# The scan's first projection moved into the tail of the soft mixture, and the late decays spread over the scan's first steps

## The chip, the cores and the metric

One core of a Trainium2 chip runs the whole program. The metric is the device time of one execution in microseconds. The kernel was timed in three runs; a fourth execution was profiled, and all rows of the trace come from that one.

## What is computed

The reference is two blocks of a network on x of shape (2, 2048, 256), in float32. Block 0 is attention and a soft mixture of experts. Block 1 is a state-space layer (Mamba-2) and an expert-choice mixture. Each is modulated by shift, scale and gate rows of a conditioning vector. What matters here is the end of the soft mixture and the beginning of the state-space layer:

```python
h = _layernorm(x) * (1 + ca) + sa          # then the layer's own norm
zxbcdt = u @ W_in + b_in                   # 1160 columns: z 512, xs 512, B 64, C 64, dt 8
dt = softplus(zxbcdt[..., -8:] + dt_bias); A = -exp(A_log)
decay = exp(dt * A)
h = decay * h + (dt * xs) B^T ; y = h C    # a scan over 2048 positions
y = (y + D * xs) * silu(z)
x = x + ga * (y @ W_out + b_out)
```

## The kernel before, in words

The work runs in 32 tiles of 128 positions, 16 for each of two batches. Each phase is one block in which every engine has its own written-out instruction list; engines wait for each other on semaphores. Between two blocks stands a barrier, at which all engines and the DMAs that the block waits for have ended.

**Soft mixture** (`soft_mixture`). For batch 1, a loop over turns t = 0 to 15 combines the experts' outputs for tile t: PE does eight products (`combine`, L1665, seen as 16 matmul records), DVE adds them into x and takes statistics (`update`, L1176 to L1181). PE may begin turn t when DVE has updated tile t-2. Between the turns the rows for the scan are made for pairs of tiles, eight pairs, numbered 0 to 7:

- DVE `row_stats` (L1189 to L1197), POOL `power` (L1037), DVE `state_rows` (L1209 to L1223) into a row buffer of the pair's parity, POOL a second power (L1046), DVE `state_offset` (L1229), ACT `state_normed` (L1469), PE `state_turn` (L1674, the transposes of the pair), ACT `state_turned` (L1482), SP `turned_out` (L971, to DRAM), PE `state_steps` (L1683, the step size matmuls), DVE `step_sizes` (L1236, which empties the buffer that the next use but one needs).
- the residual, which also uses the row buffer: POOL in three operations (L1052 to L1056, semaphore u_x) for pairs 0 to 5 of batch 1, DVE in three operations (`residual`, L1317 to L1321) for pairs 6 and 7. `state_rows` of a pair waits until the pair before the last, which has the same buffer, has its residual.
- the tail after turn 15: step matmuls of pair 4, then turn and steps of pairs 5, 6 and 7.

The decays of the scan's tiles (softplus, cumulative sums, exponentials) are made in three parts. The first 16 tiles are done in turns 0 to 5. The second part, the first two tiles of batch 1, is begun in turn 8 (`log_ratio`), turn 10 (`decay_sizes` on DVE, `cumulate` on PE, L1693), turn 13 (`keep_sums`), 14 (`turn_sums`, L1700) and 15 (`keep_turned`, L1310). The remaining 14 tiles, the "late" ones, are done in the scan's block before its loop.

**Scan** (`state_space`). Step n handles job n: tile n // 2 of batch n % 2. For each job PE does `project` (L2331 on: three outputs pbc, px, pz with 128, 512 and 512 columns, each of six exact matmuls and one for the bias, L2337), `states`, `state_rows`, `within`, `correlate` and `outputs`. ACT splits the input tile (`high`, L1979), empties the projection (`evacuate`, L1985 to L1989) and computes the decays' exponentials (`decay`, L2006 and L2009) from rows that SP fetches (`stage`, L1896 to L1898: cs, et and a broadcast of 512 KB, cumb). DVE subtracts the low half (`low`, L2107), gates, masks and updates the state. The order on each engine is written out by hand: before the loop come both first tiles, project(0) and all late decays (ACT `late_exp`, `late_log`, `late_sums`; DVE `late_ratio`, `late_sizes`, `late_kept`; PE `late_cumulate`, L2419). SP's list is: two small loads, stage(0), stage(1), the first and third quarter of uT (L1884, 1 MB each), the modulation rows (768 KB), the gate weights (L1915), three shared weight matrices (512 KB each), the other two quarters, the late cumulative sums out (L1921), and then stage(n) from n = 2. ACT negates the gate weights (L2072) before its loop. In the loop ACT's list of step n begins with high(n+2) and evacuate(n+1), and has decay(n+1) after them.

## Time and profile before

| | us |
|---|---|
| median of 3 runs | 1760.3 |
| lowest and highest run | 1756.54, 1760.31 |
| the profiled execution, from outside | 1759.81 |
| its span in the trace | 1758.1 |
| PE busy (matmul) | 1642.9, 93% |
| PE weight loads | 1383.2, 79% |
| DVE busy | 1209.1, 69% |
| ACT busy | 732.0, 42% |
| POOL busy | 544.9, 31% |

Busy time is a sum over the span; an engine's idle time costs something only where others wait for it. The mean granted clock of PE is 0.98 of its full 2.4 GHz. In the rows, a line of a timeline begins with start and duration in us; "[3.87 <-DVE d_f_dA L1294]" says that the engine was idle for 3.87 us before it and which instruction released it. SPq rows are the issues of DMAs, not the transfers.

### The profile page before, as it was taken

The page shows a single profiled execution, that of the slowest core. Times are in us where ns is not written, and L with a number is a line of the kernel's source. Part 1 is how long each engine was busy: PE and PEld are TensorE (multiplying, and loading weights), DVE is VectorE, ACT ScalarE, POOL GpSimd, SP SyncE. Part 2 cuts the span into 40 slices and gives each one's busy share as a digit, 9 for nine tenths or more (in the row PEclk, how much of TensorE's full clock was granted, in tenths as well). Part 3 has the DMA queues.
Part 4 walks back from the last instruction along what each step waited for, and adds up shares of the span by engine and source line. Part 5 has one row for each costly group of instructions (what it writes and reads, how often), then busy time and mean ns, then how long its engine had stood idle before and what let it go on. Part 6 is the DMA issues. An engine that isn't in the chain of part 4 may idle for free. (4 is left out here: it accounts for less than half of the span.)

```text
span 1758.1 us, 25512 instructions
## 1 busy us (share of the span) xinstructions
PE 1642.9 (93%) x9248; PEld 1383.2 (79%) x9248; DVE 1209.1 (69%) x2662; ACT 732.0 (42%) x1443; POOL 544.9 (31%) x446
## 2 busy tenths in 40 slices
PE   6999989989999999979987999999989999999996
PEld 4788878888867888856876888888768787888895
DVE  6877678764435655636686899999967845666663
ACT  3333333343324234424525666666621224444442
POOL 2100020000000003222252666666600023777764
PEclk9999999999999999989987999999999999999998
DMA  6000000010010000020116122232141123656553
GB/s 221 4 1 1 1 1 1 1 49 1 1 48 1 1 13 13 29 95 26 52 33 209 61 76 76 76 87 81 63 145 60 60 60 119 171 134 171 132 128 37
DMA packets 80248, 111.55 MB, mean 63 GB/s; under 512 B 15982, under 2 KB 60154, under 8 KB 79868
## 3 DMA queue, kind: packets, MB, share of 16 engines
q1 hardware_dynamic: 66172, 91.43, 16.1%
q0 software_dynamic: 12288, 17.31, 5.5%
q8 instruction: 75, 1.23, 0.3%
q10 hardware_dynamic: 1664, 1.18, 0.2%
q14 instruction: 49, 0.40, 0.1%
HBM read 81.59 MB, written 27.68 MB: 62 GB/s over the span
## 5 line engine op out<-in xcount | busy, mean ns | idle before, releaser
L2915 POOL DMA_INDIRECT out<-k_eo,idx x64 | 117.3, 1832 | 75.4 <-DVE k_eo L3007 60.7
L1816 POOL DMA_INDIRECT k_xe<-rows_dram,idx x64 | 82.5, 1289 | 178.8 <-DVE idx L2848 140.7
L1665 PE MATMUL d_pO<-d_sp,d_raw 128*128 128x257 f32 x512 | 116.6, 385 | 2.8 <-ACT d_raw L1460 2.7
L1665 PEld LDWEIGHTS d_pO<-d_sp,d_raw 128*128 128x128 f32 x512 | 96.9, 192 | 18.1 <-ACT d_raw L1460 3.5
L537 ACT ACTIVATE b_p<-b_pS,b_nmax 128x2048 f32<-128x2048 f32 (+14 forms) x32 | 40.6, 1270 | 141.2 <-DVE b_nmax L678 141.2
L61 PE MATMUL b_pO<-b_vh,b_ph 128*128 128x256 f32 x302 | 88.0, 291 | 4.4 <-DVE b_pl L660 4.3
L62 PE MATMUL b_pO<-b_vh,b_pl 128*128 128x256 f32 x302 | 85.7, 284 | 0.0
L63 PE MATMUL b_pO<-b_vl,b_ph 128*128 128x256 f32 x302 | 85.5, 283 | 0.0
L333 POOL TENSOR_TENSOR x<-x,b_vrow 128x256 f32<-128x256 f32 x32 | 24.0, 782 | 187.8 <-DVE b_hs L606 187.7
L2006 ACT ACTIVATE g_dlm<-g_cumb,g_cs 128x128 f32<-128x128 f32 x256 | 78.4, 393 | 2.5 <-DMA g_cumb<-cum_dram 2.5
L1441 ACT COPY d_raw<-d_pL 128x512 f32<-128x512 f32 x64 | 37.4, 588 | 93.4 <-PE d_pL L63 93.4
L2966 ACT ACTIVATE k_act_g<-k_pg 128x512 f32<-128x512 f32 x64 | 38.3, 598 | 88.5 <-PE k_pu L63 88.5
L61 PE MATMUL k_po<-k_wh,k_hh 128*128 128x256 f32 x256 | 72.4, 283 | 2.1 <-issue 2.1
L3020 DVE TENSOR_TENSOR k_hid<-k_act_g,k_pu 128x512 f32<-128x512 f32 x64 | 44.1, 688 | 44.1 <-ACT k_act_g L2966 43.5
L669 DVE TENSOR_REDUCE b_part<-b_pS 128x1 f32<-128x512 f32 (+3 forms) x86 | 53.1, 624 | 28.5 <-PE b_pS L63 28.2
L63 PE MATMUL k_po<-k_wl,k_hh 128*128 128x256 f32 x256 | 72.5, 283 | 0.0
L62 PE MATMUL k_po<-k_wh,k_hl 128*128 128x256 f32 x256 | 72.4, 283 | 0.0
L61 PE MATMUL b_pS<-b_kh,b_qh 128*128 128x512 f32 (+3 forms) x172 | 70.0, 407 | 1.4 <-DVE b_vl L652 1.4
L660 DVE TENSOR_TENSOR b_pl<-b_pT,b_ph 128x512 fp32r<-128x512 f32 (+3 forms) x86 | 50.4, 619 | 25.1 <-ACT b_ph L529 25.0
L1620 PE MATMUL d_pO<-o_vals,mod 128*128 128x256 f32 x256 | 63.7, 393 | 4.1 <-ACT mod L1446 4.1
L2606 ACT ACTIVATE i_act_g<-i_pg 128x512 f32<-128x512 f32 x30 | 17.9, 598 | 114.2 <-PE i_pu L63 112.1
L63 PE MATMUL b_pS<-b_kl,b_qh 128*128 128x512 f32 (+3 forms) x172 | 64.9, 377 | 0.0
(568 smaller groups left out, 5336.8 us busy)
## 6 DMA issues: line engine op xcount, KB each, us to landing
g_cumb<-cum_dram SPq DMA_DIRECT2D x32, 512.0 KB, 4.2
k_wf<-in_WgT SPq DMA_DIRECT2D x16, 512.0 KB
k_wf<-in_WuT SPq DMA_DIRECT2D x16, 512.0 KB
k_wf<-in_WdT SPq DMA_DIRECT2D x16, 512.0 KB
rows_dram<-h_hx SPq DMA_DIRECT2D x32, 136.0 KB, 3.9
x<-in_x SPq DMA_DIRECT2D x8, 512.0 KB, 9.5
d_w<-in_w SPq DMA_DIRECT2D x4, 1024.0 KB, 6.2
uT_dram<-d_ug SPq DMA_DIRECT2D x16, 256.0 KB, 2.4
```

The lines of the kernel that those rows point to most:

```text
L61: nc.tensor.matmul(out, ah, bh, start=start, stop=False)
L62: nc.tensor.matmul(out, al, bh, start=False, stop=False)
L63: return nc.tensor.matmul(out, ah, bl, start=False, stop=stop)
L537: nc.scalar.activation(pr[:, n % 2, 0:w], pS[:, bank[n]:bank[n] + w], ACT.Exp, bias=nmax[:, n % 2:n % 2 + 1], scale=scale, accum_out=esum[ ...
L660: nc.vector.tensor_tensor(pl[:, r, 0:w], src[:, 0:w], ph[:, r, 0:w].bitcast(F32), ALU.subtract).then_inc(s["lo_done"], 1)
L669: nc.vector.reduce_max(part[:, n % 2, g:g + 1], pS[:, bank[n] + g * GW:bank[n] + g * GW + width(n, g)], axis=AX).then_inc(s["part_done"], 1)
L1620: last = nc.tensor.matmul(pO[:, et % 2, 0:C], eT[g % 2][:, j * P:(j + 1) * P], xn[g * GT + j], start=g == 0 and j == 0, stop=g == NG - 1 a ...
L1665: last = nc.tensor.matmul(pO[:, t % 2, 0:PW], raw[e][:, t * P:(t + 1) * P], proc[e], start=e == 0, stop=e == E - 1)
L1816: nc.gpsimd.indirect_dma_start(out=m.xe[:, e % 2, t, :], out_offset=None, in_=m.rows, in_offset=bass.IndirectOffsetOnAxis(ap=column(m, e, ...
L2006: nc.scalar.activation(le[:, b, h, :], cumb[:, b, h, :], ACT.Relu, bias=cs[:, b, 3, h:h + 1], scale=-1.0).then_inc(s["dd_done"], 1)
L2915: nc.gpsimd.indirect_dma_start(out=out, out_offset=bass.IndirectOffsetOnAxis(ap=column(m, e, t), axis=0), in_=eo[:, e % 2, t, :], in_offse ...
L3020: nc.vector.tensor_tensor(hid[:, f % 2], act_g[:, f % 2], pu[:, f % 2], ALU.mult).then_inc(s["hid_done"], 1)
```

## The change

Four things are changed.

1. **First projection.** project(0), its split into halves, and stage(0) leave the scan. The mixture does them: ACT `first_high` after pair 3's rows, DVE `first_low` at turn 13, PE `first_projection` in three parts in the tail, one of 7 matmuls with 128 columns after pair 5's turn, one of 7 with 512 columns after pair 6's turn, one of 7 with 512 after pair 6's steps. SP issues the three DMAs of stage(0) (`first_stage`) after pair 4's turned rows. Four PSUM banks (pL) are kept for both blocks.
2. **Third row buffer.** Pair 5 of batch 1 gets a buffer of its own. Its residual moves from POOL to DVE, in three parts between the operations of the tail; pair 7's rows wait for pair 3's residual.
3. **Second part of the decays.** `cumulate` moves from turn 10 to 12, `keep_sums` from 13 to 14, `turn_sums` from 14 to 15, `keep_turned` from turn 15 into the tail.
4. **Scan.** The late decays are spread over steps 0 to 3; each projection output waits for its own buffer only; project(1) has correlate(0) between its first and second output; SP fetches the modulation rows after stage(3), and the quarters of uT, the gate weights and the shared matrices before stage(2); ACT negates the gate weights in step 3; two memsets are smaller or later.

The core of the diff:

```diff
+        first_h, first_l = [placed(n, [P, CH, P], area + k * KB, FR) for k, n in enumerate(("first_h", "first_l"))]
+        m.cumb = placed("cumb", [P, B, HEADS, P], area + 30 * KB - 512)
-        pL = ps("d_pL", [P, T])
+        pL = m.pL
+        third = placed("uh_third", [P, 2, C], area + 10 * KB)
+        rows_of = lambda b, q: third[:] if b and q == PAIRS - 3 else uh_[b][:, q % 2]
...
+            def first_stage():
+                sp.wait_ge(s["o_ready"], B * NTB)
+                sp.wait_ge(s["f_kept"], 1)
+                sp.wait_ge(s["f_out"], 16)
+                sp.wait_ge(s["f_turned"], 2)
+                sp.dma_start(m.csb[:, 0], m.cs[:, 0]).then_inc(s["bb_in"], 16)
+                sp.dma_start(m.etb[:, 0], m.etot[:, 0]).then_inc(s["bb_in"], 16)
+                sp.dma_start(m.cumb[:, 0].rearrange("p h t -> p (h t)"),
+                             m.cum_dram[0:HEADS, :].rearrange("h t -> (h t)").partition_broadcast(P)).then_inc(s["bb_in"], 16)
             for q in range(PAIRS):
                 turned_out(1, q)
+                if q == PAIRS - 4:
+                    first_stage()
...
-                    if b and q >= PAIRS - 2:
+                    if b and q >= PAIRS - 3:
                         continue
...
-                if n >= 2:
+                if b and q == PAIRS - 1:
+                    dve.wait_ge(s["u_x"], n - 3)
+                elif n >= 2:
                     dve.wait_ge(s["u_x"], n - 1)
...
-                        if t in (3, 13):
-                            keep_sums(t // 13)
-                        if t in (5, 15):
-                            keep_turned(t // 15)
+                        if t in (3, 14):
+                            keep_sums(t // 14)
+                        if t == 5:
+                            keep_turned(0)
+                        if t == 13:
+                            first_low()
...
             step_sizes(1, PAIRS - 4)
+            residual(PAIRS - 3, 0)
             state_rows(1, PAIRS - 1)
             step_sizes(1, PAIRS - 3)
+            residual(PAIRS - 3, 1)
             state_offset(1, PAIRS - 1)
+            keep_turned(1)
+            residual(PAIRS - 3, 2)
+            step_sizes(1, PAIRS - 2)
             for q in range(PAIRS - 2, PAIRS):
-                residual(q)
-                step_sizes(1, q)
+                for i in range(3):
+                    residual(q, i)
+            step_sizes(1, PAIRS - 1)
...
-                        if t in (2, 10):
-                            cumulate(t // 10)
-                        if t in (4, 14):
-                            turn_sums(t // 14)
+                        if t in (2, 12):
+                            cumulate(t // 12)
+                        if t in (4, 15):
+                            turn_sums(t // 15)
+            def first_projection(part):
+                if part == 0:
+                    pe.wait_ge(s["winl"], CH + 1)
+                    pe.wait_ge(s["winh"], CH + 3)
+                    pe.wait_ge(s["f_cumT"], 1)
+                    pe.wait_ge(s["f_kept"], 2)
+                bank_of, o, width = ((2, ZX, 2 * STATE), (1, INNER, INNER), (0, 0, INNER))[part]
+                dst = pL[:, bank_of * GW:bank_of * GW + width]
+                for k in range(CH):
+                    exact_matmul(nc, dst, first_h[:, k, :], first_l[:, k, :], m.winh[:, k, o:o + width], m.winl[:, k, o:o + width], k == 0, False)
+                nc.tensor.matmul(dst, m.onesr[:], m.bb[:, o:o + width], start=False, stop=True)
             for kind, q in tail:
                 if kind == "u":
                     state_turn(1, q)
+                    if q < PAIRS - 1:
+                        first_projection(q - PAIRS + 3)
                 else:
                     state_steps(1, q)
+                    if q == PAIRS - 2:
+                        first_projection(2)
@@ scan, SP @@
-            stage(0)
             stage(1)
             inputs(0)
             inputs(2)
-            sp.wait_ge(s["f_chain"], 9)
-            sp.dma_start(m.mod[:, :, SB:GB + 1, :].rearrange("p b m c -> p b (m c)"),
-                         m.mod_dram[1][:, SB:GB + 1, :].rearrange("b m c -> b (m c)").partition_broadcast(P)).then_inc(s["mods_in"], 16)
             sp.dma_start(gw[:], w["gate_wT"].rearrange("(h p) n -> p h n", p=P)).then_inc(s["gate_in"], 16)
             for dst, src in ((m.wg, w["Ws_gT"]), (m.wu, w["Ws_uT"]), (m.wd, w["Ws_dT"])):
                 sp.dma_start(dst[:], src.rearrange("(h p) n -> p h n", p=P)).then_inc(s["shared_in"], 16)
             inputs(1)
             inputs(3)
+            stage(2)
+            stage(3)
+            sp.wait_ge(s["f_chain"], 9)
+            sp.dma_start(m.mod[:, :, SB:GB + 1, :].rearrange("p b m c -> p b (m c)"),
+                         m.mod_dram[1][:, SB:GB + 1, :].rearrange("b m c -> b (m c)").partition_broadcast(P)).then_inc(s["mods_in"], 16)
+            stage(4)
             sp.wait_ge(s["f_cumT"], 1)
             sp.dma_start(m.cum_dram[late.start * HEADS:late.stop * HEADS, :], cumT[0:NL, :]).then_inc(s["f_out"], 16)
-            for n in range(2, LAST):
+            for n in range(5, LAST):
@@ scan, ACT @@
-            high(0)
             high(1)
-            late_exp()
-            late_log()
-            decay(0)
             act.wait_ge(s["zeroed"], 1)
             evacuate(0)
             by_state(0)
-            late_sums()
-            act.wait_ge(s["gate_in"], 16)
-            nc.scalar.mul(minus_gw[:], gw[:], -1.0).then_inc(s["gate_done"], 1)
+            decay(0)
+            late_exp()
             for n in range(LAST):
...
+                if n == 2:
+                    late_sums()
                 if is_job(n + 1):
                     decay(n + 1)
+                if n == 1:
+                    late_log()
+                if n == 3:
+                    negated_gate()
@@ scan, DVE @@
-            low(0)
             low(1)
-            late_ratio()
-            late_sizes()
+            nc.vector.memset(H[:], 0.0)
             gates(0)
+            nc.vector.memset(by_tile, 0.0)
             masked(0)
-            late_kept()
             for n in range(LAST):
-                if n == 1:
-                    late_turned()
...
+                if n == 2:
+                    late_kept()
                 if is_job(n):
                     sums(n)
+                if n == 3:
+                    late_turned()
...
+                if n == 0:
+                    late_ratio()
+                if n == 1:
+                    late_sizes()
@@ scan, PE @@
-                pe.wait_ge(s["ul_done"], n + 1)
-                pe.wait_ge(s["bc_copied"], n)
-                pe.wait_ge(s["zr_done"], n)
-                pe.wait_ge(s["xs_copied"], n)
-                for dst, o, width in ((pbc, ZX, 2 * STATE), (px, INNER, INNER), (pz, 0, INNER)):
+                pe.wait_ge(s["ul_done"], n)
+                for dst, o, width, freed in ((pbc, ZX, 2 * STATE, "bc_copied"), (px, INNER, INNER, "xs_copied"), (pz, 0, INNER, "zr_done")):
+                    pe.wait_ge(s[freed], n)
+                    if n == 4 and freed == "bc_copied":
+                        pe.wait_ge(s["f_kept"], 1)
+                    if n == 1 and freed == "xs_copied":
+                        correlate(0)
...
-            project(0)
-            late_cumulate()
             await_bc(0)
             state_rows(0)
-            correlate(0)
             for n in range(LAST):
                 if is_job(n + 1):
                     project(n + 1)
-                if n == 0:
-                    late_turn()
-                if n == 1:
-                    pe.wait_ge(s["f_cumT"], 1)
+                if n == 2:
+                    late_cumulate()
...
                     states(n)
+                if n == 3:
+                    late_turn()
```

## Rows read from the trace of the kernel before

**Rows 1.** Busy time by stretch: us, PE, PEld, DVE, ACT, POOL, granted clock, DMA share, GB/s
```profile
845.00:917.00 72.00, 67.69 (x334) 58.82 (x334) 60.71 (x192) 22.68 (x43) 35.27 (x32) 0.95 0.10 31
917.00:934.00 17.00, 7.53 (x33) 6.62 (x32) 11.11 (x40) 5.45 (x11) 2.15 (x4) 0.55 0.14 48
934.00:957.00 23.00, 17.96 (x81) 13.93 (x82) 13.21 (x29) 13.79 (x38) 6.58 (x6) 0.81 0.85 294
957.00:987.00 30.00, 30.00 (x191) 25.05 (x190) 25.79 (x43) 18.98 (x49) 17.34 (x17) 1.00 0.29 95
```
**Rows 2.** Timeline of PE from turn 10 to the tail: start, duration, instruction, idle before
```profile
893.01 0.61 PE L1693 MATMUL d_pL<-d_f_dA,d_upto 128*128 128x16 f32 x2 [3.87 <-DVE d_f_dA L1294]
...
912.15 3.64 PE L1665 MATMUL d_pO<-d_sp,d_raw 128*128 128x257 f32 x16
915.64 0.95 PE L1683 MATMUL d_pT<-mod,d_ug 128*128 128x8 f32 x8
...
921.14 1.88 PE L1683 MATMUL d_pT<-mod,d_ug 128*128 128x8 f32 x8 [4.06 <-DVE mod L1236]
```
**Rows 3.** Groups of DVE instructions, 893.9 to 920.9: busy, mean ns, idle before
```profile
L1176 DVE RECIPROCAL d_crs<-d_pO 128x1 f32<-128x1 f32 x5 | 0.8, 162 | 3.1 <-PE d_pO L1665 3.1
```
**Rows 4.** Timeline of DVE, rows of pairs 6 and 7
```profile
913.31 2.61 DVE L1209 SCALAR_TENSOR_TENSOR d_uh<-x,mean,d_umod 128x256 f32<-128x256 f32 x2
...
918.72 0.28 DVE L1310 COPY d_cumT<-d_pL 16x128 f32<-16x128 f32 x1
...
921.80 0.88 DVE L1209 SCALAR_TENSOR_TENSOR d_uh<-x,mean,d_umod 128x256 f32<-128x256 f32 x2 [0.72 <-issue]
...
924.47 0.17 DVE L1236 TENSOR_TENSOR mod<-d_pT,mod 128x16 f32<-128x16 f32 x1
925.37 0.16 DVE L1229 SCALAR_TENSOR_TENSOR mod<-mod 128x2 f32<-128x2 f32 x1 [0.72 <-POOL mod L1046]
925.45 0.68 DVE L1317 TENSOR_TENSOR d_uh<-d_uh,d_ubout 128x512 f32<-128x512 f32 x1
```
**Rows 5.** Timeline of POOL, residual of pair 5, second of three operations
```profile
914.31 1.33 POOL L1054 TENSOR_TENSOR d_uh<-d_uh,d_umod 128x512 f32<-128x512 f32 x1
```
**Rows 6.** Timeline of SP's DMA issues over the border
```profile
929.04 0.51 SPq L971 DMA_DIRECT2D uT_dram<-d_ug  x1
933.79 0.35 SPq L1878 DMA_DIRECT2D g_neg<-in_A_log  x1
...
938.28 1.22 SPq L1884 DMA_DIRECT2D uT<-uT_dram  x2
```
**Rows 7.** Timeline of PE, the scan's start
```profile
936.13 0.47 PE L61 MATMUL g_pbc<-d_winh,g_uh 128*128 128x128 f32 x1 [5.13 <-DVE g_ul L2107]
...
943.27 0.37 PE L2419 MATMUL g_py<-g_fdA,d_upto 128*128 128x112 f32 x2
...
956.57 0.30 PE L61 MATMUL g_pbc<-d_winh,g_uh 128*128 128x128 f32 x1 [0.30 <-DVE g_wide L2112]
...
960.68 0.60 PE L2358 MATMUL g_pyT<-ident,g_wide 128*128 128x128 f32 x4
...
966.47 0.22 PE L61 MATMUL g_pbc<-d_winh,g_uh 128*128 128x128 f32 x1
```
**Rows 8.** Timeline of ACT, the scan's start
```profile
936.55 1.28 ACT L2039 ACT_TABLE_LOAD   x1
...
952.16 0.23 ACT L2072 ACTIVATE h_mgw<-h_gw 128x32 f32<-128x32 f32 x1 [5.95 <-DMA h_gw<-in_gate_wT]
...
964.70 2.46 ACT L2006 ACTIVATE g_dlm<-g_cumb,g_cs 128x128 f32<-128x128 f32 x8 [1.08 <-DMA g_cumb<-cum_dram]
```
**Rows 9.** Timeline of DVE, the last of the four late size operations
```profile
939.59 0.28 DVE L2222 SCALAR_TENSOR_TENSOR g_fdA<-d_cs,g_neg 128x112 f32<-128x112 f32 x1
```
**Rows 10.** Instructions on tile uT, 930 to 975: its four loads
```profile
DMA to landing us min/median/max: 7.0/11.9/14.4
```
**Rows 11.** The page's DMA issues: count, KB each, median us to landing
```profile
g_cumb<-cum_dram SPq DMA_DIRECT2D x32, 512.0 KB, 4.2
```

79 lines of the change are left out of this document (52 added, 27 removed).

## The prediction

> **What bounds the kernel now.** I went from the stretches to the engines' timelines around the border between the soft mixture and the scan, because every edit lies there. The stretches [rows 1] show the late turns of the mixture (845 to 917) with PE busy 67.7 of 72 us and DVE 60.7, the border (917 to 934) with PE busy 7.5 of 17 us at a granted clock of 0.55, the scan's start (934 to 957) with PE at 18.0 of 23 us, a clock of 0.81 and the DMA engines at 0.85 and 294 GB/s, and then the scan proper with PE busy 30.0 of 30. So PE is the bound of the scan and nothing there can be won by better order; the 40 us between 917 and 957 are where time is loose.
>
> The PE timeline [rows 2] shows two waits before the border: 3.87 us until 893.01 (the decay sums of turn 10 wait for DVE's step sizes) and 4.06 us until 921.14 (the step size matmuls of pair 5 wait until DVE has emptied the buffer of pair 4, L1236). Behind the second stands DVE's lateness, so I read DVE. From 893.9 to 920.9 it was idle 3.1 us, all of it ahead of L1176 waiting for PE's combinations [rows 3], which are late because of the first PE wait. And pair 6's rows (L1209 to L1223) took from 913.31 to 918.72, 5.41 us, while POOL ran the residual of pair 5 [rows 4, 5]; pair 7's same work, with POOL at rest, took from 921.80 to 924.47, 2.67 us.
>
> The border itself ends with a DMA: the last turned rows are issued at 929.04 and the next block's first instruction comes at 933.79 [rows 6]. Call that moment S. From S, PE starts project(0) at 936.13, begins the late sums at 943.27, and begins project(2) at 956.57 [rows 7]: 22.8 us after S. From there steps follow at PE's pace.
>
> **The change, part by part.** A: turns 10 to 15. Cumulate moves from turn 10 to 12, so PE no longer waits at 893.01; its three pairs of matmuls (0.61 for the first [rows 2], estimated 1.3 together) stay. DVE's idle 3.1 us goes, if PE keeps ahead: it can begin turn 11's combination near 891, and five combinations at 3.5 (912.15 to 915.64 [rows 2]) with two pair turns, one set of step matmuls and the sums are some 21 us, so turn 15's is ready near 912; DVE comes to it near 913. Pair 5's residual leaves POOL (that is what the third buffer allows: pair 7 waits for pair 3 instead of 5), so pair 6's rows run at pair 7's price: 5.41 - 2.67 = 2.7 us less. The first tile's low half costs DVE an estimated 0.4 us (128x256; 0.68 for 128x512 [rows 4]), the copy that moved (0.28, 0.2 of it not overlapped [rows 4]) leaves. Sum for A: -3.1 - 2.7 + 0.4 - 0.2 = **-5.6 us** until pair 7's rows begin. ACT's first high half is about as long and free, since ACT is busy 22.7 of those 72 us [rows 1]; without that cover it is 0.4.
>
> B: the tail (921.80 to S). DVE has nine residual thirds of 0.68 us [rows 4] where it had six. The first two new ones fill the two waits of 0.72 us [rows 4] for POOL's powers; the third, with the moved copy, adds 0.9 us behind the offset of pair 7, where DVE has slack until the last step sizes. PE gets the first projection: 7 matmuls of 128 columns and 14 of 512, 4.1 us in all at the full clock (project(2), 956.57 to 960.68 [rows 7]). Parts 0 and 1 lie in PE's waits for DVE (4.06 us before 921.14 [rows 2], and the time until the next step sizes). Part 2 stands before pair 7's turn and delays it by some 0.4 us, which the faster clock gives back (the step matmuls cost 1.88 us at the lower of its two levels, 1.2 GHz, and 0.95 at the upper, 2.4 GHz [rows 2]). SP issues three more DMAs after turn 15 (1.7 us), ahead of pair 5's turned rows, which are not ready then. I take **0** for B; with the clock at its lower level it is +5 (rival 1).
>
> C: from S to project(2), before 22.8 us. Gone are project(0), the late sums and the three DMA issues of stage 0. What ends last now? ACT's queue is high(2), then evacuate(1); high(2) needs the first quarter of uT. That DMA was issued 4.5 us after S behind eight others, 0.56 each [rows 6]; with three fewer it goes out at S + 2.8. Its kind took 7.0 us at least, 11.9 in the middle [rows 10]; it is the first of four, so I take 7.0: S + 9.8. PE's project(1) starts near S + 1.5 behind two small transposes, at the lower clock it takes 7 us (project(0) did, from 936.13 to 943.27 [rows 7]): S + 9. So the DMA ends last by a little. From high(2) to project(2) it was 4.4 us before (952.16 to 956.57, where ACT had waited 5.95 us for the gate weights [rows 8], a wait that the moved negation takes off this place). Project(2) then starts at S + 14.2: **-8.6 us**. Ends: -9.4 if the quarter lands sooner, since PE's projection then ends last, and -3.7 if it takes 11.9.
>
> D: the late decays in steps 0 to 3. DVE's seven ratio operations (some 2 us) fall in step 0, where it waits for PE. The sizes (four of 0.28, 1.2 in all [rows 9]) end step 1 and wait for ACT's logarithm, which is queued behind decay(2), and that waits for stage 2's rows. Stage 2 is now issued behind all four quarters of uT and three weight matrices, 6.1 MB; at 294 GB/s [rows 1] they are through some 21 us after S + 2, that is 9 us after project(2) starts. Its rows land then, or in the usual 4.2 us [rows 11], so decay(2) starts 7 to 9.6 us after project(2) (8.1 before, 964.70 [rows 8]), takes 2.46 and an exponential of 1, then the table load 1.28 and the logarithm 0.3: the sizes are ready 13.4 to 15.9 us after project(2) starts. Late cumulate stands behind project(3), which starts 9.9 and ends 14.0 us after project(2) starts [rows 7]. PE waits 0 to 1.9 us and spends some 0.9 (three pairs, 0.37 for the first [rows 7], with the next operation's start). Step 2's kept sums (0.9 on DVE) hold project(4) up to 0.5 us more. The late rows go out at the end of step 3, so stage 5 comes some 5 us later than now; ACT and DVE have 3 us of slack there. Sum for D: +1.4 to +3.6, taken at **+2.4**.
>
> On the table load, the row shows 1.28 us at 936.55 and ACT's next operation at once behind it [rows 8]. The Trainium skill (ScalarE: Activation LUTs, What ACT_TABLE_LOAD costs) adds a drain of 1.38 us to each switch of sets; by that, D would be 1.4 us more and the total 1749.4. No row here shows such a drain, so the sum goes without it.
>
> A + B + C + D = -5.6 + 0 - 8.6 + 2.4 = -11.8. The profiled execution took 1759.81 us outside and 1758.1 in its span, 0.5 under the median of 1760.3; 1759.8 - 11.8 = **1748.0**.
>
> **Rivals.** 1. The clock falls in the tail all the same. For: it fell to 0.55 there [rows 1] after a wait, and the new waits of about 1 us between projection parts remain. Against: three parts fill most of the idle time. Then parts 1 and 2 take 3 us each and stand before pair 6's steps and pair 7's turn, and B is +5: 1753.
>
> 2. PE's wait at turn 10 only moves. For: cumulate now stands behind pair 3's steps, and pair 5 of the mixture's rows on DVE is still slowed by POOL. Against: the step sizes it needs are written at turn 10, two turns earlier. DVE keeps its 3.1 us of idle and A is -2.5: 1751. That is the case in which this edit doesn't do what it says.
>
> 3. The quarter of uT lands at the middle of its kind, 11.9 us, or stage 2 sits behind the bulk as long again: C is -3.7: 1753. The Trainium skill (DMA: Bandwidth & Descriptors, Queues, rings and completion order) says that an engine takes descriptors in ring order, which would put stage 2 behind the bulk; the sum above already reaches to that end.
>
> 4. The removal of POOL's residual gives nothing. The rows show L1209's two operations at 2.61 us beside POOL's and 0.88 without [rows 4, 5], which is one instance of each. The mechanism would have to be another (the memory of x, say), and A would be -2.9: 1750.7. The Trainium skill (Perfetto Trace Analysis, Optimizing Scalar/DVE Operations) says that GpSimd and VectorE share a read port, so that moving work between the two might not help; by that warning the gain would be nothing, by the rows it is 2.7.
>
> 5. Slower than before. PE arrives in the scan cold and, with project(0) gone, waits for the late quarter of uT in step 0 so long that it stays at the lower clock through the first three steps. A step holds 9.9 us of PE (956.57 to 966.47 [rows 7]); matmuls at the lower clock took twice as long [rows 2], with waits between them less, so each such step costs 7 to 8 us. The point from which it decides is two and a half steps: then C's loss to -3.7 and +22 give 1775. Against: the granted clock averaged 0.81 from 934 to 957 and 1.00 from 957 on [rows 1], though PE came cold and waited there before too.
>
> **How the numbers follow.** Forecast 0.60, rival 1 0.12, rival 2 0.08, rival 3 0.10, rival 4 0.05, slower 0.05. A measurement of this kernel tells about 0.3%, 5.3 us, from no change: faster is below 1755.0, slower above 1765.6. The forecast's own ends are -15.1 (A 1.5 better, C at -9.4, D at +1.4) and -8.0 (C at -6, D at +3.6). Two rivals together land between 1755 and 1759, so some 0.10 falls within 0.3%. The range that holds 8 in 10 is 1743 to 1756: the lower end is 1.7 below the best sum for a B that gains, the upper takes in rivals 1 to 4 and part of their pairs.
>
> **What would show it.** In the profile after: no wait of PE over 1.5 us at turns 10 to 12; L1209 and L1214 for pair 6 below 0.9 us for two; the last turned rows issued near 923.4 instead of 929.04; a clock of 1.0 until the border (rival 1 if 0.5); project(2) some 14 us after the block's start, and ACT there waiting for uT and not for the gate weights; a PE wait of up to 2 us ahead of the late sums behind project(3); the rest of the scan at 9.9 us and more a step as before. If S comes not at least 4 us earlier, A is wrong; if project(2) comes later than S + 17, C is.

## The result and the profile after

The kernel after took 1755.8 us in the median of its 15 runs (1750.4 to 1761.5), the kernel before 1760.3 in 15 runs beside it (1756.5 to 1766.5): a ratio of 0.9972, with a 95% interval of 0.9960 to 0.9985. That is 4.5 us less where 12.3 were forecast (1760.3 to 1748.0). The profiled execution of the kernel after took 1755.81 outside and 1754.0 in its span.

The stretches of the kernel after, in the columns of [rows 1], with the edges moved to its own border:

```profile
845.00:917.00 72.00, 68.57 (x349) 59.64 (x349) 63.65 (x212) 24.56 (x46) 33.03 (x31) 0.98 0.12 39
917.00:931.00 14.00, 9.60 (x39) 7.52 (x39) 8.59 (x22) 3.16 (x7) 1.30 (x2) 0.67 0.17 58
931.00:945.00 14.00, 12.25 (x53) 9.79 (x54) 8.43 (x13) 9.61 (x29) 6.11 (x6) 0.72 0.78 275
945.00:965.00 20.00, 16.15 (x90) 13.02 (x90) 14.02 (x30) 10.06 (x23) 7.78 (x10) 0.94 0.55 200
```

The border is 14 us long instead of 17, and the scan's start is shorter; but from 945 to 965, right behind the start of project(2), PE is busy 16.15 of 20 us, where before it was busy all the time behind the start of project(2) (30.0 of 30 us from 957 on [rows 1]). There a large part of the gain is given back.

Absolute times before turn 9 differ by some us between executions of the same kernel, so I set one mark there, the start of output_low(1) in turn 9 (889.00 before, 888.50 after), and read each stage from it. Stages in us; S is the first DMA issue of the scan block, "states(1)" PE's first matmul of it, "last" PE's last matmul g_pi<-g_H of the scan:

```
                     mark to      pair 7's   S to       states(1)  mark
                     pair 7's     rows       states(1)  to last    to last
                     rows         to S
before                32.80       11.99      27.33      310.12     382.24
after                 28.74       13.90      17.95      317.93     378.52
after, profiled again 28.74       13.89      19.13      315.58     377.34
difference (first)    -4.06       +1.91      -9.38      +7.81       -3.72
difference (again)    -4.06       +1.90      -8.20      +5.46       -4.90
forecast (A B C D)    -5.6         0         -8.6       +2.4       -11.8
```

The stages give -3.7 in one execution and -4.9 in the other, the median of all runs -4.5. They account for the result. The first two stages repeat within 0.03 us in every execution whose code is the same there. The last two do not: S to states(1) moved by 1.2 us and states(1) to the last by 2.4 between the two executions of the kernel after. Now the four parts in the rows.

**Part A.** One of DVE's groups in the kernel after, 893.9 to 917.2 (busy, mean ns, idle before), against [rows 3]:

```profile
L1193 DVE RECIPROCAL d_crs<-d_pO 128x1 f32<-128x1 f32 x5 | 0.8, 159 | 0.0
```

and DVE's timeline, against [rows 4]:

```profile
901.83 1.88 DVE L1228 SCALAR_TENSOR_TENSOR d_uh_third<-x,mean,d_umod 128x256 f32<-128x256 f32 x2
903.63 2.90 DVE L1233 SCALAR_TENSOR_TENSOR d_uh_third<-d_uh_third,rstd,d_umod 128x256 f32<-128x256 f32 x2
...
907.52 0.42 DVE L1279 TENSOR_TENSOR d_first_l<-d_u,d_first_h 128x256 fp32r<-128x256 f32 x1
...
911.17 0.86 DVE L1228 SCALAR_TENSOR_TENSOR d_uh<-x,mean,d_umod 128x256 f32<-128x256 f32 x2
911.95 0.87 DVE L1233 SCALAR_TENSOR_TENSOR d_uh<-d_uh,rstd,d_umod 128x256 f32<-128x256 f32 x2
...
915.91 0.68 DVE L1342 TENSOR_TENSOR d_uh_third<-d_uh_third,d_ubout 128x512 f32<-128x512 f32 x1
917.24 0.88 DVE L1228 SCALAR_TENSOR_TENSOR d_uh<-x,mean,d_umod 128x256 f32<-128x256 f32 x2 [0.66 <-issue]
```

The 3.1 us of idle time ahead of the combinations are 0.0, and pair 6's rows take 2.65 us (911.17 to 913.82) instead of 5.41. Both are as forecast. But pair 5's rows, one pair earlier, now take 5.69 us (901.83 to 907.52); they took 4.33 before. DVE comes to them earlier and meets the whole of POOL's residual of pair 4:

```profile
901.99 1.44 POOL L1069 TENSOR_TENSOR d_uh<-d_uh,d_ubout 128x512 f32<-128x512 f32 x1 [0.50 <-ACT d_un L1504]
903.50 1.33 POOL L1071 TENSOR_TENSOR d_uh<-d_uh,d_umod 128x512 f32<-128x512 f32 x1
904.91 1.33 POOL L1073 TENSOR_TENSOR x<-x,d_uh 128x512 f32<-128x512 f32 x1
```

PE's wait of 3.87 us [rows 2] is gone, but one of 1.75 stands ahead of turn 11's combination, which needs DVE's update of turn 9:

```profile
890.38 5.43 PE L1706 MATMUL d_pO<-d_sp,d_raw 128*128 128x257 f32 x16 [1.75 <-DVE x L1195]
```

**Part B.** PE's timeline of the kernel after in the tail:

```profile
916.05 1.06 PE L1724 MATMUL d_pT<-mod,d_ug 128*128 128x8 f32 x8 [1.58 <-DVE mod L1255]
...
918.11 0.48 PE L63 MATMUL pL<-d_winl,d_first_h 128*128 128x512 f32 x1
918.38 0.63 PE L61 MATMUL pL<-d_winh,d_first_h 128*128 128x512 f32 x1
...
920.14 1.87 PE L1724 MATMUL d_pT<-mod,d_ug 128*128 128x8 f32 x8
...
924.57 0.63 PE L1826 MATMUL pL<-d_bb,d_onesr 128*128 128x512 f32 x1
925.00 0.65 PE L1715 MATMUL d_pT<-ident,d_un 128*128 128x128 f32 x4
926.85 1.03 PE L1724 MATMUL d_pT<-mod,d_ug 128*128 128x8 f32 x8 [1.20 <-ACT d_ug L1517]
```

The clock fell at 918.3, in the middle of the 512 wide part, though PE was working; matmuls of 512 columns go from 0.48 to 0.63 us there. Before, it fell at 918.8, 1.7 us into PE's wait of 4.06 [rows 2]; here PE had waited 1.58 ahead of pair 5's steps, two operations earlier. The third part (921.86 to 925.0) runs at 1.2 GHz and holds pair 7's turn behind it.

**Part C.** ACT, and the first load of uT, now end S to project(2):

```profile
940.80 0.40 ACT L2040 CAST g_uh<-uT 128x256 fp32r<-128x256 f32 x1 [3.69 <-DMA uT<-uT_dram]
```

S is 931.14, so the quarter lands at S + 9.7; the forecast said 9.8. Project(2) starts at 944.55, S + 13.4. In the second execution the quarter landed at S + 10.8.

**Part D.** ACT and PE of the kernel after in steps 1 and 2, one fence for each:

```profile
956.09 2.45 ACT L2069 ACTIVATE g_dlm<-d_cumb,mod 128x128 f32<-128x128 f32 x8 [4.49 <-DMA d_cumb<-cum_dram]
958.57 1.06 ACT L2072 ACTIVATE g_dlm<-g_dlm 128x1024 f32<-128x1024 f32 x1
959.64 1.28 ACT L2106 ACT_TABLE_LOAD   x1
960.94 0.30 ACT L2106 ACTIVATE g_fl<-g_fu 128x112 f32<-128x112 f32 x1
```

```profile
958.28 0.40 PE L2410 MATMUL pL<-d_bb,d_onesr 128*128 128x512 f32 x1
962.53 0.69 PE L2492 MATMUL pL<-g_fdA,d_upto 128*128 128x112 f32 x2 [3.85 <-DVE g_fdA L2288]
...
964.14 1.12 PE L2431 MATMUL g_pyT<-ident,g_wide 128*128 128x128 f32 x4
965.05 1.52 PE L2439 MATMUL g_pi<-g_H,g_bcT 128*128 128x512 f32 x2
966.41 1.02 PE L2444 MATMUL g_pst<-g_wide,mod 128*128 128x512 f32 x2
```

This is a chain: the rows of stage 2 land at 956.1, decay(2) starts, the table is loaded for the logarithm, DVE forms the sizes, and PE has waited 3.85 us when the late sums can start. Then the wait costs once more: the sums and what follows run at the lower clock until some 966.4 (the turn takes 1.12 instead of 0.60 us, the states 1.52 instead of 1.02). The rows of stage 2 come late behind the bulk that SP issued ahead of them (the first experiment tests this); the loads of the tile d_cumb from 931 to 975:

```profile
DMA to landing us min/median/max: 3.7/4.0/11.2
```

### The profile page after: what moved, and what is told of

Read it like the earlier page. It is cut to its first block and busy times, and to the rows that moved or that the text cites. A ratio compares the mean times of both kernels' runs of the same rounds, so it can differ in the third digit from the quotient of the medians.

```text
span 1754.0 us, 25485 instructions
## 1 busy us (share of the span) xinstructions
PE 1642.5 (94%) x9248; PEld 1381.3 (79%) x9248; DVE 1207.4 (69%) x2665; ACT 731.8 (42%) x1443; POOL 541.2 (31%) x443
## 3 DMA queue, kind: packets, MB, share of 16 engines
q10 hardware_dynamic: 1664, 1.18, 0.2%
## 5 line engine op out<-in xcount | busy, mean ns | idle before, releaser
L2069 ACT ACTIVATE g_dlm<-d_cumb,mod 128x128 f32<-128x128 f32 x256 | 78.5, 394 | 4.7 <-DMA d_cumb<-cum_dram 4.7
L1476 ACT COPY d_raw<-pL 128x512 f32<-128x512 f32 x64 | 37.3, 587 | 93.3 <-PE pL L63 93.3
L61 PE MATMUL pL<-d_winh,g_uh 128*128 128x128 f32 (+1 forms) x186 | 68.4, 368 | 0.2 <-DVE d_cs L2296 0.2
L63 PE MATMUL pL<-d_winl,g_uh 128*128 128x128 f32 (+1 forms) x186 | 67.0, 360 | 0.0
```

Source lines behind the costliest of these rows:

```text
L61: nc.tensor.matmul(out, ah, bh, start=start, stop=False)
L63: return nc.tensor.matmul(out, ah, bl, start=False, stop=stop)
L2069: nc.scalar.activation(le[:, b, h, :], cumb[:, b, h, :], ACT.Relu, bias=cs[:, b, 3, h:h + 1], scale=-1.0).then_inc(s["dd_done"], 1)
```

## The experiments

The theory from the two traces: D is the term that was wrong, by the landing of stage 2's rows (W), and B by the lower clock in the tail (T). Rivals: the serial chain behind the landing (decay, table load, logarithm) is the cost whenever the rows land; and C owes its gain to the negation of the gate that moved, not to the projection. All stages below are read in the same way as in the table above.

### Stage 2 ahead of the bulk, and the logarithm ahead of decay(2)

```diff
+            stage(2)
             for dst, src in ((m.wg, w["Ws_gT"]), ...):
                 sp.dma_start(...)
             inputs(1)
             inputs(3)
-            stage(2)
```

> The changed kernel with one edit: stage(2) is issued ahead of the shared weights and the last two quarters of uT. Theory W (the 4.49 us that ACT's decay(2) waited for cumb comes from 3.5 MB queued ahead of it, and PE's 3.85 us wait before the late sums comes from that): decay(2) starts at once after the turned states, near 951.6 instead of 956.09; the logarithm is done near 956.7; no PE wait before the late sums and no fall of the clock behind it (1.6 us); project(4) comes 5 to 6 us earlier, the median near 1750. Rival (the wait is only the logarithm's place in ACT's queue, and rows land late however they are ordered): project(4) moves by less than 1 us, 1755.

```diff
+                if n == 1:
+                    late_log()
                 if is_job(n + 1):
                     decay(n + 1)
-                if n == 1:
-                    late_log()
```

> The changed kernel with one edit: in step 1 ACT takes the logarithm before decay(2) instead of after it. Theory W says that it is then free of the DMA: logarithm near 953.2, sizes on DVE at the end of step 1 near 957.6, no PE wait before the late sums; decay(2) still waits for cumb until 956.1 and now needs another table load, so weigh(2) ends near 962.3 and PE waits 0.5 us or more before within(2). Gain 4 to 5 us, the median near 1751. If instead PE's time is lost by DVE or by the clock alone, it stays at 1755.

And the two together:

> Both edits of the two kernels before. If both remove the same wait (theory W), they do not add: 5 to 6.5 us under the changed kernel, the median 1749 to 1751. If the two were separate losses, they would add to some 10 us, 1746.

```
                     S to       states(1)  mark      median   ratio to before,
                     states(1)  to last    to last            95% interval
after                17.95      317.93     378.52    1755.8   0.9972 (0.9960 to 0.9985)
stage 2 first        18.92      313.21     374.78    1756.3   0.9968 (0.9954 to 0.9981)
logarithm first      18.81      313.87     375.30    1754.2   0.9958 (0.9944 to 0.9973)
both                 19.48      313.25     375.37    1755.0   0.9964 (0.9951 to 0.9977)
```

With stage 2 first the DMA wait on ACT and the wait of PE are gone, and the sums and what follows run at the upper clock. ACT, then PE:

```profile
957.31 0.37 ACT L2062 COPY g_bcT<-pL 128x256 f32<-128x256 f32 x1 [0.64 <-PE pL L2415]
957.58 2.44 ACT L2069 ACTIVATE g_dlm<-d_cumb,mod 128x128 f32<-128x128 f32 x8
```

```profile
965.67 0.37 PE L2492 MATMUL pL<-g_fdA,d_upto 128*128 128x112 f32 x2
...
966.52 0.66 PE L2431 MATMUL g_pyT<-ident,g_wide 128*128 128x128 f32 x4
967.02 1.02 PE L2439 MATMUL g_pi<-g_H,g_bcT 128*128 128x512 f32 x2
```

and the slowest landing of the tile in its first 40 us is 5.8 us, where it was 11.2:

```profile
DMA to landing us min/median/max: 3.8/4.5/5.8
```

States(1) to the last states comes down by 4.7 us (by 2.4 against the second execution of the kernel after, in which the rows landed earlier and PE waited 1.85). The logarithm ahead of decay(2) takes a part of the same chain away (PE waits 1.42 us instead of 3.85) and brings 4.1. The two together bring 4.7, no more than the first: they work on one wait, they don't add. So the landing is the cause, and the chain behind it decides only once the landing is late.

What the runs don't show is that gain in the median. The three expectations said 1749 to 1751; the medians are 1754.2 to 1756.3, so all three missed. Against the kernel after, the four intervals overlap: the ratios say that stage 2 first gains 0.7 us and the other two 2.5 and 1.4, and each interval is some 5 us wide. The stages up to the last states say 3.2 to 3.7 us against its first execution and 2.0 to 2.6 against its second. Executions vary in what the edits don't touch: S to states(1) by 1.5 us with the landing of uT, the time ahead of the mark by 6 (887.45 to 893.60), and the time behind the last states by 5 (486.4 to 491.5).

### The gate's negation, in the kernel before

```diff
-            act.wait_ge(s["gate_in"], 16)
-            nc.scalar.mul(minus_gw[:], gw[:], -1.0).then_inc(s["gate_done"], 1)
             for n in range(LAST):
...
+                if n == 3:
+                    act.wait_ge(s["gate_in"], 16)
+                    nc.scalar.mul(minus_gw[:], gw[:], -1.0).then_inc(s["gate_done"], 1)
```

> The kernel before with one edit: ACT negates the gate weights in step 3 instead of before the loop. It measures what this part of the change gives by itself. If the first quarter of uT had landed by 951, evacuate(1) follows project(1) at once and project(2) comes 1.2 us earlier (955.4); if it had not, less; the span then 1757 to 1758.1.

S to states(1) is 25.46 us against 27.33: this move alone is worth 1.9 of C's 9.4, more than the 1.2 expected. The other 7.5 are left for the projection and the late work that went, and for the three DMA issues; no run here separates these. The other stages come again within 0.03 us. The span, 1757 to 1758.1 in the expectation, was 1761.2: behind the last states this execution took 491.5 us where the one before took 486.9, in code that the edit doesn't touch. That is why these experiments are read from stages.

### The tail: order and place of the parts

```diff
-                    if q < PAIRS - 1:
-                        first_projection(q - PAIRS + 3)
+                    first_projection(q - PAIRS + 3)
                 else:
                     state_steps(1, q)
-                    if q == PAIRS - 2:
-                        first_projection(2)
```

> The changed kernel with the third part of the projection behind pair 7's turn instead of ahead of it. Times are counted from the start of turn 11's combination, since the phases before it differ by some us from run to run. Theory T (the border's loss of 2 us against my sum is the third part at the lower clock, standing ahead of pair 7's turn): the turn follows ACT's rows at once, 2.3 us earlier, the last rows go out 2.3 us earlier and the scan's block begins 1.4 to 1.9 us earlier. Rival (the block's end is set by DVE's residual and step sizes): it begins less than 0.8 us earlier.

```diff
-                bank_of, o, width = ((2, ZX, 2 * STATE), (1, INNER, INNER), (0, 0, INNER))[part]
+                bank_of, o, width = ((1, INNER, INNER), (2, ZX, 2 * STATE), (0, 0, INNER))[part]
```

> The changed kernel with the first two parts exchanged: 512 columns behind pair 5's turn, where PE then waited 1.58 us, and 128 behind pair 6's. If that wait is what lets the clock fall in the second part, the part at 917 to 922 keeps the upper level (0.95 for pair 6's step matmuls instead of 1.87), and the block begins 1.5 to 2.5 us earlier. If the clock falls all the same, it begins within 1 us of the changed kernel's 40.8 us after turn 11's start.

The third part behind pair 7's turn brings the last issue of turned rows 1.86 us forward, and S 0.88 (41.76 us behind the mark, from 42.64). That is less than the 1.4 to 1.9 expected and just above the rival's 0.8: the last step matmuls now stand behind the third part and take 1.71 us. The order of the first two parts changes nothing at S (42.68), as its second expectation has it. It also speaks against the wait as what lets the clock fall: PE waited 0.70 us instead of 1.58 ahead of pair 5's steps, and the clock fell 29.84 us behind the mark, in the kernel after 29.76. Pair 6's steps took 1.87 us again, and part 2 still runs at 0.63 us a matmul.

### The sums at turn 10 again, and the residual on POOL again

```diff
-                        if t in (2, 12):
-                            cumulate(t // 12)
+                        if t in (2, 10):
+                            cumulate(t // 10)
```

> The changed kernel with cumulate back behind turn 10. My sum A says that DVE gets its idle 3.1 us back: measured from turn 9's update on DVE, pair 7's rows begin 2.5 to 3.1 us later than in the changed kernel, and the block too. Rival 2 of the prediction (the wait only moves): under 1 us.

```diff
-                    if b and q >= PAIRS - 3:
+                    if b and q >= PAIRS - 2:
                         continue
...
-            residual(PAIRS - 3, 0)
-            residual(PAIRS - 3, 1)
-            residual(PAIRS - 3, 2)
```

> The changed kernel with pair 5's residual back on POOL (it keeps the third buffer). By my sum pair 6's rows take 5.4 us again instead of 2.65 and pair 7's rows begin 2.7 us later; the three residual parts leave DVE's tail. Rival 4 (the two rows' difference had another cause): pair 6's rows stay under 3.2 us.

With the sums at turn 10 PE's wait is back:

```profile
892.27 0.61 PE L1734 MATMUL pL<-d_f_dA,d_upto 128*128 128x16 f32 x2 [3.86 <-DVE d_f_dA L1318]
```

Pair 7's rows begin 1.65 us later, and S comes 0.18 us earlier (42.46). Both miss the expectation (2.5 to 3.1 us later). Pair 5's rows take 4.32 us here, so moving the sums to turn 12 won 3.1 us of idle time and lost 1.4 in them. The tail's later rows say why S is no later: the clock fell at the same place (29.80 us behind the mark) but was back 3.4 us sooner, for the steps of pair 6 (1.87 us in the kernel after) and for the whole of part 2, so what DVE lost PE got back:

```profile
922.14 0.96 PE L1724 MATMUL d_pT<-mod,d_ug 128*128 128x8 f32 x8
922.95 0.48 PE L61 MATMUL pL<-d_winh,d_first_h 128*128 128x512 f32 x1
```

From pair 6's turn to the start of pair 7's steps PE takes 7.65 us here (918.79 to 926.44) and 9.67 in the kernel after (917.18 to 926.85), with the same work: the lower clock costs 2.0 there. So the 3.1 us that DVE won are, at the border, worth nothing. In the other kernel, with the residual on POOL, pair 6's rows take 5.73 us again (5.4 expected), and pair 7's begin 2.55 later (2.7 expected):

```profile
911.92 2.93 DVE L1228 SCALAR_TENSOR_TENSOR d_uh<-x,mean,d_umod 128x256 f32<-128x256 f32 x2
914.78 1.88 DVE L1233 SCALAR_TENSOR_TENSOR d_uh<-d_uh,rstd,d_umod 128x256 f32<-128x256 f32 x2
```

and S is 2.42 us later (45.06). Yet from the mark to the last states this kernel takes 378.54 us, against 378.52. The stages of the four kernels, one execution each:

```
                     mark   S to       states(1)  mark      time
                     to S   states(1)  to last    to last   (one run)
after                42.64  17.95      317.93     378.52
third part last      41.76  21.36      312.15     375.27    1752.7
wide part first      42.68  23.02      312.10     377.80    1757.8
sums at turn 10      42.46  20.36      313.92     376.74    1755.2
residual on POOL     45.06  21.35      312.13     378.54    1756.4
```

It would be easy to read 378.54 and 378.52 as a later border that was hidden in the wait for stage 2. The stages say otherwise: +2.42 at the border, +3.40 up to states(1), -5.80 behind it. In this kernel the clock was at 1.2 GHz from S + 12.1 to S + 18.9, so project(2) ran slowly (its first matmul 0.45 us, 0.31 in the kernel after). When ACT came to decay(2) the rows of stage 2 had just landed (S + 23.7), so it didn't wait for them, and PE didn't wait ahead of the late sums, which ran at the upper clock:

```profile
949.28 0.45 PE L61 MATMUL pL<-d_winh,g_uh 128*128 128x128 f32 x1
...
965.09 0.37 PE L2489 MATMUL pL<-g_fdA,d_upto 128*128 128x112 f32 x2
```

```profile
958.08 2.45 ACT L2066 ACTIVATE g_dlm<-d_cumb,mod 128x128 f32<-128x128 f32 x8
```

Where project(2) ran at the lower clock (the third part last, the wide part first, the residual on POOL), states(1) to the last states is 312.1 with stage 2 still in its late place. One loss stands in for the other, and the total says nothing about either. Nor could a later border hide in that wait: the rows landed 24.9 and 24.1 us behind S in the two executions of the kernel after, 25.0 with the sums at turn 10 and 23.7 here, so a later S brings them later too.

### With the wait for stage 2 gone

Two edits on top of "stage 2 first": the residual on POOL as above; and the ratio moved into step 0's wait for uT. The four profiles of this section come from another chip than those of the experiments above. The expectation that follows takes the equal totals for a loss that was hidden.

> Stage(2) first, and pair 5's residual back on POOL. With stage(2) in its late place the residual's return cost 2.4 us at the border (start of the scan block 45.06 us behind turn 9's output_low instead of 42.64) and nothing at the last states (378.54 against 378.52). Theory (the wait for stage(2)'s rows takes in whatever is lost ahead of it, so part A's second half was real but hidden): with the rows early the loss reaches the end, turn 9 to the last states 376.5 to 377.5, where the kernel with stage(2) first has 374.8. Rival (the scan's first steps have another slack of their own, and the tail's 2.4 us never count): 374.5 to 375.3.

```diff
             for n in range(LAST):
+                if n == 0:
+                    late_log()
                 if is_job(n + 2):
                     high(n + 2)
...
-                if n == 1:
-                    late_log()
...
+                if n == 0:
+                    late_ratio()
                 if is_job(n + 2):
                     low(n + 2)
...
                 if n == 0:
-                    late_ratio()
-                if n == 1:
                     late_sizes()
```

> The kernel after with stage(2) issued first, and the late decays' elementwise work moved once more: the seven operations of the ratio on DVE go between weigh(0) and low(2), the logarithm on ACT stands before high(2), the four operations of the sizes take the ratio's old place at the end of step 0; the sums stay in step 2. Theory (what is left of part D in the kernel with stage(2) first, 3.1 us more than before from states(1) to the last states, is partly the 3.3 us of the ratio that push DVE's step 1 and make outputs(1) wait 0.82 us for y_low): in step 0 DVE and ACT wait 3.7 to 3.9 us for the quarters of uT in any case, so the ratio costs nothing there, and states(1) to the last states comes down from 313.2 to about 312.3, turn 9 to the last states from 374.8 to 373.9; the idle time before outputs(1) goes. Rival (the uT wait is shorter than ratio plus logarithm in a run where uT lands early, or the path runs through ACT's table loads): states(1) itself comes 0.5 to 1.5 us later, or nothing changes, and turn 9 to the last states stays at 374.8 or above.

Then both useful edits with the tail's new order, and the kernel after once more:

> The three edits that each had a reason in the trace, together: stage(2) first, the ratio in the wait of step 0, and the third part of the first projection behind pair 7's turn. If the tail's order gains 0.9 us at the border (as it did by itself) and that is no longer swallowed by the wait for stage(2)'s rows, turn 9 to the last states is 373.0, about 1.8 below the kernel with stage(2) first alone and 5.5 below the kernel after; in the median about 1754 against 1756. Rival (the gain at the border is taken back by a fall of the clock in step 0, as when PE sat idle before outputs in the kernels with an earlier border): S to states(1) is 2 to 4 us longer, and turn 9 to the last states stays between 374.5 and 376.

> The kernel after, unchanged, profiled once more: how much the stages vary from one execution to the next. If the times from turn 9 on are the kernel's own, its stages come again within 0.5 us (border 42.6 us, S to states(1) 17.9, states(1) to the last states 317.9), and PE's granted clock stays at 2.4 GHz in project(2). If which step of the scan meets the lower clock is a matter of the execution, S to states(1) can be 2 to 4 us longer (as in the kernels with one part moved) with states(1) to states(2) shorter by as much, and the sum to the last states still 378 to 379.

```
                         mark   S to       states(1)  mark      median
                         to S   states(1)  to last    to last
after                    42.64  17.95      317.93     378.52    1755.8
after, again             42.63  19.13      315.58     377.34    1754.9 (one run)
stage 2 first            42.65  18.92      313.21     374.78    1756.3
 + residual on POOL      45.04  17.86      313.19     376.09    1752.4 (one run)
 + ratio in step 0       42.63  18.36      312.20     373.19    1751.0 (5 runs)
 + third part last too   41.76  23.55      312.07     377.38    1752.7 (10 runs)
```

**The residual.** States(1) to the last states is 313.19 against 313.21, so the later border of 2.39 us is passed on; S to states(1) is 1.06 shorter, since uT landed 1.04 sooner behind S in that execution. The total, 376.09, lies between the two expectations. The residual's move to DVE is then worth 2.4 us. It does not show that the wait for stage 2 had hidden them: with that wait in place the loss reached S as well (2.42), and it was the low clock of project(2) that changed the rest.

**The ratio.** DVE and ACT now do it and the logarithm in the wait for uT, and the expectation (312.3) is met with 312.20. The wait of 0.82 us ahead of outputs(1) is gone. ACT:

```profile
937.63 1.28 ACT L2106 ACT_TABLE_LOAD   x1
938.97 0.30 ACT L2106 ACTIVATE g_fl<-g_fu 128x112 f32<-128x112 f32 x1
941.72 0.40 ACT L2040 CAST g_uh<-uT 128x256 fp32r<-128x256 f32 x1 [2.45 <-DMA uT<-uT_dram]
```

This is the best kernel of the study: 1751.0 us (1750.2 to 1752.1 in 5 runs), 0.9940 of before (0.9919 to 0.9961), and 5.3 us less from the mark to the last states than the kernel after (4.2 less than its second execution). Its interval just touches that of the kernel after (0.9960 to 0.9985).

**The three edits.** The border comes 0.88 us earlier, as alone, and S to states(1) takes 5.2 us longer. The stretches S to S + 4, to 10, to 14 and to 20 show it, with the ratio in step 0 first and the third part last too in the second fence (columns as in [rows 1]):

```profile
931.65:935.65 4.00, 3.25 (x13) 3.07 (x14) 2.71 (x6) 3.98 (x13) 0.96 (x1) 0.50 0.22 60
935.65:941.65 6.00, 5.45 (x15) 3.67 (x13) 3.78 (x8) 3.48 (x7) 2.08 (x3) 0.70 0.98 357
941.65:945.65 4.00, 3.26 (x24) 2.76 (x24) 3.46 (x5) 3.90 (x9) 2.79 (x3) 1.00 0.22 75
945.65:951.65 6.00, 6.00 (x30) 4.42 (x29) 5.77 (x11) 4.73 (x12) 3.03 (x3) 1.00 0.68 227
```

```profile
932.52:936.52 4.00, 3.25 (x13) 3.08 (x14) 2.72 (x6) 3.98 (x13) 0.96 (x1) 0.50 0.23 62
936.52:942.52 6.00, 4.34 (x15) 2.85 (x13) 3.79 (x8) 3.48 (x7) 2.09 (x3) 0.91 0.95 336
942.52:946.52 4.00, 2.89 (x12) 2.31 (x12) 3.09 (x5) 3.53 (x8) 2.43 (x2) 0.74 0.30 104
946.52:952.52 6.00, 6.00 (x24) 5.54 (x24) 4.23 (x9) 3.35 (x9) 2.33 (x3) 0.50 0.71 192
```

The clock comes back sooner (0.91 against 0.70 in the second stretch), PE is through with project(1) sooner, waits longer for uT (2.77 us, 1.29 in the other), and the clock falls again at 944.5, 0.9 us behind that wait and 4.3 ahead of project(2). So the rival came about in kind, with more than its price: 5.2 us up to states(1) where it said 2 to 4, and 377.38 in all, outside the forecast and the rival. One thing limits this: the profiled execution (1758.16 us) is the longest of this kernel's ten, of which six took 1749.3 to 1753.1 and four 1756.9 to 1758.2. What the clock did in the other nine is not shown. The same is seen in the other kernels. Where the tail was unchanged (after and its second execution, stage 2 first, logarithm first, both, ratio in step 0), the clock came back late in project(1), PE waited 0.86 to 2.42 us before step 0's states, and the clock held, six times of six. In five others the clock came back 2.3 to 3.4 us sooner behind S and fell again for 3.4 to 10.2 us, after waits of 2.11 (residual), 2.20 (third part last), 2.66 (wide part first), 2.77 (three edits) and 3.06 (sums at turn 10, where it was back before project(2)). The sixth, with a wait of 1.85 (stage 2 first, residual on POOL), held. The lengths of the waits overlap (2.42 held, 2.11 didn't), so the wait alone doesn't decide; why it falls is not shown.

**The kernel after again.** The border came again (42.63), and project(2) ran at 2.4 GHz. The other two stages did not come again within the 0.5 us expected: +1.18 and -2.35, and the total of 377.34 lies under the 378 to 379 of the alternative too. So a difference of 1 to 2 us in these two stages between single executions is no finding.

## Why the prediction was right and wrong

**A, -5.6 forecast, -4.06 measured.** Both mechanisms were right and each had its size on DVE (3.1 of idle time gone, 2.76 of pair 6's rows). What failed is the step that took these as the whole: pair 5's rows were left at their old price, and they became 1.36 dearer since DVE reached them while POOL worked on pair 4's residual. Rival 4 fell (moving the residual back costs 2.6 us at pair 7's rows). Rival 2 fell too: DVE's idle time went. PE's wait did not go whole, though: 1.75 us stand at turn 11, over the 1.5 that the prediction allowed there.

**B, 0 forecast, +1.91 measured.** Rival 1 came about in kind, at 2 of its 5 us. The clock fell at 918.3 with PE at work, so the second half of part 1, the steps of pair 6 and part 2 ran at 1.2 GHz. But the last steps ran at the upper clock (1.03 us, before 1.84), which I had offered as compensation and rival 1 had not. My sentence that the clock "gives back" what part 2 delays was wrong: of A's gain the border kept 2.15 us, and by the prediction's own sign (S at least 4 us earlier) the part up to S had failed. The kernel with the sums at turn 10 shows the size: with part 2 at the upper clock pair 7's rows to S take 12.07 us, 0.08 more than before, which is the forecast's 0.

**C, -8.6 forecast, -9.38 measured.** Right, step by step: the load of uT ended last, S + 9.7 against 9.8; rival 3's half on uT did not happen. That it came so near has some luck in it, since in the second execution the quarter landed 1.1 us later and C was -8.20. The clock was back before project(2). Rival 5 needed it at the lower level for two steps and a half; four of the other kernels had project(2) at the lower clock, for 6.8 to 10.2 us, which is about one step, and none came near its price.

**D, +2.4 forecast, +7.81 measured.** This is the step that failed. I let stage 2's rows land "9 us after project(2) starts" by dividing 6.1 MB by 294 GB/s; they landed 11.5 us after (956.09 to 944.55), in the second execution 9.6, which is the late end of my 7 to 9.6. I then let PE wait "0 to 1.9 us". It waited 3.85, and 1.85 in the second. Two things were outside the sum: (1) the rate of [rows 1] was a mean over a stretch and I started it at S + 2, while the loads of the second half of uT were issued only from S + 7; (2) after the wait the clock fell, so that sums priced at 0.9 took 1.61 and the two operations behind them about 1 more. Together with the wait that is 6.4 of the 7.8 us. The range was added wrongly as well: its terms (0 to 1.9, 0.9, up to 0.5) give 0.9 to 3.3, not 1.4 to 3.6. Stage 2 first takes away 4.7. What is left then (3.1) has another part that I had laid in DVE's wait for PE: the ratio at the end of step 0 pushes DVE, PE waits 0.82 ahead of outputs(1), and moving the ratio brings 1.0. In the kernel after that wait isn't there, so the ratio is no term of its 7.8. Of the last 2.1 the three sums are 0.9, the step behind them 0.5, and 0.6 is spread over all the later ones; why these are longer is not shown. The second half of rival 3, stage 2 behind the bulk, is the one that came. I had named it and then put its price inside the forecast's range, where it should have stood with its own chance.

The Trainium skill (DMA: Bandwidth & Descriptors, Queues, rings and completion order) has descriptors taken in ring order. The landing of 11.2 us behind the bulk and 5.8 at most ahead of it agrees. The other sentence that I weighed, of the Trainium skill (ScalarE: Activation LUTs, What ACT_TABLE_LOAD costs), puts a drain of 1.38 us on each switch of sets. It is not borne out here: the load of 1.28 at 959.64 begins as the exponential ends and the logarithm follows 0.02 behind it.

**The sum.** -4.06 + 1.91 - 9.38 + 7.81 = -3.72. The error of 8.1 is 5.4 in D, 1.9 in B, 1.5 in A, and -0.8 in C. The sign held, and the median of 1755.8 lies at the upper end of the range of 1743 to 1756; the point did not hold. Rivals 1 and 3 came about together, each in part, for which the prediction had named 1755 to 1759.

What stays open: whether the gain of the kernels with stage 2 first is real in the median. By their stages they are 2 to 4 us faster than the kernel after, by the ratios of all runs not to be told from it. A fall of the clock in project(2) in some executions would explain it, but none was profiled in those kernels.

## What to carry to other kernels

When work is moved out of a start that was bound by transfers, look at the next transfer in SP's order, not at the engine's next instruction: here half a MB that was due soon stood behind 5.5 MB, part of which was not, and moving one call ahead of it gave back 4.7 us (2.4 against the second execution) in the stage that it feeds. When two kernels take the same time, read the stages before you say that a gain was hidden: here +2.42, +3.40 and -5.80 made 0.02. Profile the same kernel twice before you price an edit of 1 or 2 us. And a piece of work that an engine is given to keep it busy has to be counted with the clock that it leaves behind for the next stage.

## What was not expected of the hardware

- The granted clock fell at 918.3 in the middle of seven matmuls of 512 columns issued without a gap, after a wait of 1.58 us two operations earlier. In all fourteen executions profiled here it fell 29.7 to 29.9 us behind the mark, whatever PE had done there: idle (before), behind a wait of 0.70 us (the wide part first), behind one of 0.47 (the sums at turn 10). So no order of the tail that was tried moved the fall; when it came back did change.
- A clock that came back 2.3 to 3.4 us sooner behind S was followed by a new fall in five executions of six. The order of the tail that made the border 0.88 us earlier had project(2) at 1.2 GHz both times: with stage 2 in its late place states(1) came 3.4 us later behind S and the total was 3.3 us less than in the kernel after (2.1 less than in its second execution); with stage 2 early it came 5.2 later and the total was 4.2 more than without that order (in the longest of its ten runs).
- The pair of 128x256 operations that DVE does on a pair's rows took 0.86 to 0.88 us with POOL at rest and, beside POOL's 128x512 operations, up to 2.93. Pair 5's rows took 4.32 us with the sums at turn 10 and 5.69 with them at turn 12, wherever the residual of pair 5 was: with the sums at turn 12 DVE came to them 2.8 us earlier and met all three of POOL's operations.
